# Mixture-of-experts loop: one group of small matmuls per tile, transposes and third weights a tile ahead, routing weights in a row per tile

## The chip, the cores and the metric

One core of a Trainium2 chip. The metric is the device time of one execution in microseconds, median of several runs. The engines that matter are TensorE (PE in the rows, with its weight loads as PEld), VectorE (DVE), ScalarE (ACT) and GpSimd (POOL); SyncE (SP) issues the DMAs. Each engine works through its own list of instructions in order and meets the others at semaphores.

## The reference

Cut to what matters. `x` is 2 x 1024 rows of 256.

```python
x = x + cross_attention(layernorm(x), ctx, ctx, mask)      # 16 heads, 64 keys
# second half, on xf = layernorm(x), 2048 rows:
xa = xf @ P_w.T
C1, C2, C3 = (route(xa, U) for U in (U1, U2, U3))          # per row: softmax of the 3 largest of 12 logits, else 0
mixture = lambda inp, C, W: sum(C[:, e:e+1] * (inp @ W[e].T) for e in range(12))
h = gelu(mixture(xf, C1, W1))
x = x + mixture(h, C2, W2) + C3 @ b2
```

## The kernel before

The 2048 rows are 16 tiles of 128 (T = 16). A first part computes the attention of all tiles and splits the expert weights into a high and a low part of type float32r (`w_h`, `w_l`); a second part, the expert loop, begins some 134 us into the span and is what the change is about. Order and waits are written out by hand, engine by engine; nothing is scheduled by a compiler.

Each product with an expert's weights is made of three matmuls (high x high, low x high, high x low) over two halves of the 256 inputs, six matmuls of 512 columns for two experts at once (a "pair", `expert_pairs`, `split_product`). A layer of a tile has six pairs, so 36 such matmuls; they go to six banks of PSUM in turn. The stationary operand is the tile transposed and split: `xf_h`, `xf_l` for layer 1, `h_h`, `h_l` for layer 2 (the last tile's h goes to `xf_h`, `xf_l`). VectorE multiplies each half bank with its column of routing weights and adds it up (`sum_pair`, L810 and L815: 12 instructions a layer), so a bank is free again once VectorE has read it (semaphore `acc`).

An iteration `experts(t)` on TensorE is: layer 1 of tile t+1, then layer 2 of tile t. Beside the 72 large matmuls it holds small ones in float32, in three places:

- after three pairs of layer 1: two transposes of h(t) (`transpose_h`, L1043) and one of the third routing weights (`transpose_c3`, L1050);
- after six pairs: the bias product with these weights (`expert_bias`, L1055) and two transposes of xf(t+2) (`transpose_xf`, L1025);
- after three pairs of layer 2: the routing logits of tile t+2 (`logits`, L1035: two matmuls, four rows in the trace).

Transposes of h and of xf share one PSUM range, `ps_t`. ScalarE copies the transposes out as high parts (L561, L491, L493), VectorE makes the low parts (`h_low` L751, `xf_low` L746), and TensorE waits for `xf_lo` before layer 1 and for `h_lo` before layer 2.

VectorE, beside the products: `statistics` and `normalise2` of tile t+2 (L595 to L598, L602), `find_top` (L757 to L768: top three and their indices), `combine_weights` (L774 to L793: the dense rows of weights, into `c_new`), `move_weights` (L801: `c_new` to `c_cur`, which layer 2 reads while `c_new` is written anew). GpSimd: `inverse_deviation` (L355, L357: the 1/deviation that `normalise2` waits for), `exponentials` (L406), `split_c3` (L417, L422).

The loop runs over t = 1 to 13 as a hardware loop; t = 0 and t = 14 and the last layer are written out. Inside it, semaphore values and tile offsets are computed in registers by the engine's sequencer (REGISTER_ALU and ISA rows in the order, ALU_OP and FUSED_REGOPS in the trace).

Every on-chip tensor starts at a multiple of 32 bytes, in the order of the declarations. Within 64 bytes `w_h`, `w_l`, `xf_h` and `xf_l` start at 32, `h_h` and `h_l` at 0.

Of the kernel before, what the change touches and what calls it, by code (L numbers as in the profile page):

```python
# [5 lines left out]
ALU = mybir.AluOpType  # L6
# [8 lines left out]
P = 128  # L15
# [6 lines left out]
def xattn_ffn_kernel(nc: bass.Bass, x, mask, ctx_t, wq_t, bq, wk_t, bk, wv_t, bv, wo_t, bo,  # L22
# [56 lines left out]
    with ExitStack() as ctx:  # L79
# [30 lines left out]
        waited = sb("waited", [P, 1])  # L110
        euler = sb("euler", [P, 3 * TOP_K])
# [49 lines left out]
        c_new = sb("c_new", [P, 3, EXPERTS])  # L161
        c_cur = sb("c_cur", [P, 3, EXPERTS])
# [22 lines left out]
        ps_t = banks[:, 5, 0:D].rearrange("p (c t) -> p c t", c=C)  # L185
# [32 lines left out]
        def weights2(t):  # L218

            return c_new if is_last(t) else c_cur  # L220

# [42 lines left out]
        c_moved = sem("c_moved")  # L264
# [56 lines left out]
        def _(pool):  # L321
# [87 lines left out]
            def split_c3(t):  # L409

                if is_last(t):
                    pool.wait_ge(route, ROUTE_STEPS * T)
                else:
                    pool.wait_ge(c_moved, t + 1)
                if later(t, 1):
                    pool.wait_ge(c3t_done, t)
                pool.tensor_tensor(c3_hlh[:, 0:3:2, 0:EXPERTS].bitcast(F32R),  # L417
                                   weights2(t)[:, 2:3, :].to_broadcast([P, 2, EXPERTS]),
                                   ones[:, 0:2 * EXPERTS].rearrange("p (k e) -> p k e", k=2),
                                   ALU.mult).then_inc(c3_hi, 1)  # L420
                pool.wait_ge(c3_hi, t + 1)
                pool.tensor_tensor(c3_hlh[:, 1, 0:EXPERTS], weights2(t)[:, 2, :], c3_hlh[:, 0, 0:EXPERTS],  # L422
                                   ALU.subtract).then_inc(c3_lo, 1)

            exponentials(0)
            inverse_deviation(1, stats2_ready, var2_ready, rstd2_ready)
            exponentials(1)
            split_c3(0)
            with pool.Fori(2, T) as t:
                inverse_deviation(t, stats2_ready, var2_ready, rstd2_ready)  # L430
                exponentials(t)
                split_c3(t - 1)
            split_c3(T - 1)


        @block.scalar
        def _(act):
# [47 lines left out]
            def copy_xf(t):  # L485
# [5 lines left out]
                nc.scalar.activation(xf_t[:, :, :], ps_t, ACT.Copy).then_inc(xf_copied, 1)  # L491
                act.wait_ge(xf_copied, t + 1)
                nc.scalar.activation(xf_h[:, :, :], xf_t[:, :, :], ACT.Copy).then_inc(xf_hi, 1)  # L493
# [55 lines left out]
            copy_xf(0)  # L549
            copy_pt(T - 2)  # L550
# [5 lines left out]
            copy_xf(1)  # L556


            def h_high(t):
                act.wait_ge(ht_done, t + 1)  # L560
                nc.scalar.activation(h_buffers(t)[0][:, :, :], ps_t, ACT.Copy).then_inc(h_hi, 1)  # L561

            def copy_c3t(t):
                act.wait_ge(c3t_done, t + 1)
                nc.scalar.activation(c3_t[:, :], ps_c3, ACT.Copy).then_inc(c3t_copied, 1)
# [7 lines left out]
            gelu(0, SUMS)  # L573

            def experts(t):
# [5 lines left out]
            experts(0)  # L581
            with act.Fori(1, T - 2) as t:
                experts(t)
            h_high(T - 2)
            copy_c3t(T - 2)
            gelu(T - 1, SUMS * 2 * (T - 1))
            h_high(T - 1)
            copy_c3t(T - 1)
# [3 lines left out]
        def _(dve):  # L592
# [155 lines left out]
            def h_low(t):  # L748
                dve.wait_ge(h_hi, t + 1)
                high, low = h_buffers(t)  # L750
                dve.tensor_tensor(low[:, :, :], ps_t, high[:, :, :].bitcast(F32), ALU.subtract).then_inc(h_lo, 1)  # L751

            def find_top(t):

                n = ROUTE_STEPS * t
                dve.wait_ge(z_done, t + 1)
                dve.tensor_copy(z_sb[:, :, :].rearrange("p r e -> p (r e)"), ps_z).then_inc(route, 1)  # L757
# [12 lines left out]
            def combine_weights(t):  # L770
# [20 lines left out]
                if later(t, 1):  # L791
                    dve.wait_ge(c_moved, t)
                dve.tensor_reduce(c_new[:, :, :], w_at_e[:, :, :, :], AX_X, ALU.add).then_inc(route, 1)  # L793

            def move_weights(t):

                dve.wait_ge(route, ROUTE_STEPS * (t + 1))
                if later(t, 1):
                    dve.wait_ge(c3t_done, t)
                    dve.wait_ge(acc, SUMS * (2 * t + 1))  # L800
                dve.tensor_copy(c_cur[:, :, :], c_new[:, :, :]).then_inc(c_moved, 1)  # L801
# [20 lines left out]
            def layer1_pairs(t, pairs, last=True):  # L822
                for pair in pairs:
# [4 lines left out]
                    sum_pair(slot1(t), pair, c_new[:, 0, :], sum1, 0)  # L828
# [3 lines left out]
            def start_layer2(t):  # L832

                dve.wait_ge(y_done, t + 1)
                if is_last(t):
# [3 lines left out]
                if not is_last(t):  # L839
                    dve.wait_ge(c_moved, t + 1)  # L840

            def layer2_pairs(t, pairs):
                for pair in pairs:
                    sum_pair(slot2(t), pair, weights2(t)[:, 1, :], sum2, 1)
# [23 lines left out]
            layer1_pairs(0, range(0, 2))  # L868
            a_low(T - 2)
# [13 lines left out]
            def experts(t, ahead=True):  # L883
                if ahead:
                    statistics(t + 2, x_all, bn2_done, stats2_ready)
# [325 lines left out]
```

## Time and profile before

| | us |
|---|---|
| median of 3 runs | 414.63 (414.23 to 415.75) |
| span of the profiled execution | 412.4 |
| PE busy in it | 392.4 (95%) |
| DVE busy | 342.9 (83%) |
| ACT busy | 115.8 (28%) |
| POOL busy | 110.9 (27%) |

The clock granted to TensorE is full in nearly every slice of the page. Times in the rows are us from the start of the span. A row of the timeline is: start, duration, engine, line, operation, written<-read, count, and in brackets the idle time of the engine before it with what ended it. Instructions overlap on an engine, so the step from one start to the next start is what an instruction takes from the engine's time.

### The profile page before, as it was taken

Reading aid. Unit: us, or ns where it says so; the run is one execution under the profiler, and the core shown is the slowest. Engines: PE = TensorE matmul, PEld = TensorE weight load, DVE = VectorE, ACT = ScalarE, POOL = GpSimd, SP = SyncE. Lnnn points to the kernel's source line nnn. Section 1 sums busy time; section 2 is a strip of 40 time slices with the busy share of each in tenths; the row PEclk is TensorE's granted clock in tenths of the full one; section 3 lists DMA queues with packets and bytes.
Section 4 is the critical chain, followed back from the end, with each engine's and each line's share of the span. In section 5 each row is a group of like instructions: output and inputs, shape, how many; then the busy total and the mean of one; then the engine's idle time right before and its main releaser. Section 6 shows DMA issues by size and latency. Waiting matters only on the chain.

```text
span 412.4 us, 7824 instructions
## 1 busy us (share of the span) xinstructions
PE 392.4 (95%) x2132; PEld 331.0 (80%) x2132; DVE 342.9 (83%) x1036; ACT 115.8 (28%) x263; POOL 110.9 (27%) x165
## 2 busy tenths in 40 slices
PE   4499999999989999999999999999999999999996
PEld 4388988989868888888888888888888888888884
DVE  3998889889885889789897988989789898888875
ACT  3477888888822111010110101011010100101000
POOL 5462755657520220202112020211202112020200
PEclk9999999999989999999999999999999999999999
DMA  7900123131000000000000000000000000000000
GB/s 225 333 2 2 61 92 98 55 102 51 2 0 3 0 2 13 13 0 13 0 13 13 0 13 0 13 0 13 13 0 13 0 13 13 0 13 0 14 0 26
DMA packets 8612, 12.71 MB, mean 31 GB/s; under 512 B 1076, under 2 KB 5016, under 8 KB 8472
## 3 DMA queue, kind: packets, MB, share of 16 engines
q1 hardware_dynamic: 8040, 12.44, 9.1%
q10 hardware_dynamic: 560, 0.13, 0.1%
q8 instruction: 5, 0.08, 0.1%
q14 instruction: 7, 0.06, 0.0%
HBM read 10.47 MB, written 2.10 MB: 30 GB/s over the span
## 4 chain that ended last, share of the span: by engine, by line
PE 89%; DVE 4%; issue 3%; ACT 2%; DMA 1%; POOL 1%; ACTq 0%; DVEq 0%; POOLq 0%
PE banks L920 68%; PE banks L997 5%; PE banks L987 3%; PE banks L962 3%; PE banks L972 2%; PE banks L975 2%; PE banks L977 2%; PE banks L1035 1%; DMA bk_sb<-in_bk_dram 1%; PE banks L1043 1%; DVE q_hl L625 1%; PE banks L1025 1%; PE banks L1008 1%; PE banks L953 1%; DVE s_max L631 1%
## 5 line engine op out<-in xcount | busy, mean ns | idle before, releaser
L815 DVE SCALAR_TENSOR_TENSOR s_d<-banks,c_cur,s_d 128x256 f32<-128x256 f32 x165 | 72.7, 478 | 27.6 <-PE banks L920 23.1
L920 PE MATMUL banks<-w_h,xf_h 128*128 128x512 f32 x204 | 81.8, 401 | 0.0
L920 PE MATMUL banks<-w_l,xf_h 128*128 128x512 f32 x204 | 80.6, 395 | 0.0
L920 PE MATMUL banks<-w_h,xf_l 128*128 128x512 f32 x204 | 80.2, 393 | 0.0
L406 POOL TENSOR_TENSOR top_e<-euler,top_d 128x9 f32<-128x9 f32 x16 | 28.9, 1807 | 185.1 <-DVE top_d L765 185.1
L920 PE MATMUL banks<-w_h,h_h 128*128 128x512 f32 x180 | 73.5, 408 | 0.0
L920 PE MATMUL banks<-w_l,h_h 128*128 128x512 f32 x180 | 71.1, 395 | 0.0
L920 PE MATMUL banks<-w_h,h_l 128*128 128x512 f32 x180 | 71.1, 395 | 0.0
L815 DVE SCALAR_TENSOR_TENSOR sum<-banks,c_new,sum 128x256 f32<-128x256 f32 x160 | 66.6, 476 | 3.2 <-PE banks L920 3.1
L561 ACT ACTIVATE h_h<-banks 128x256 fp32r<-128x256 f32 x15 | 5.8, 385 | 156.5 <-PE banks L1043 156.5
L920 PEld LDWEIGHTS banks<-w_l,xf_h 128*128 128x128 f32 x204 | 38.6, 189 | 8.5
L920 PEld LDWEIGHTS banks<-w_h,xf_l 128*128 128x128 f32 x204 | 38.8, 190 | 7.8
L920 PEld LDWEIGHTS banks<-w_h,xf_h 128*128 128x128 f32 x204 | 38.8, 190 | 7.7
L920 PEld LDWEIGHTS banks<-w_l,h_h 128*128 128x128 f32 x180 | 33.8, 188 | 8.2
L920 PEld LDWEIGHTS banks<-w_h,h_l 128*128 128x128 f32 x180 | 33.9, 188 | 6.9
L920 PEld LDWEIGHTS banks<-w_h,h_h 128*128 128x128 f32 x180 | 33.9, 188 | 6.8
L366 POOL TENSOR_TENSOR w_l<-stage,w_h 128x1024 f32 (+1 forms) x12 | 28.8, 2397 | 32.6 <-ACT w_h L534 32.6
L997 PE MATMUL banks<-v_ext,prob_t 128*128 (+1 forms) x256 | 30.1, 273 | 0.5 <-ACT prob_t L476 0.5
L997 PEld LDWEIGHTS banks<-v_ext,prob_t 128*128 128x128 f32 x256 | 29.9, 192 | 0.7 <-issue 0.7
L571 ACT ACTIVATE xn_t<-xn 128x256 f32<-128x256 f32 x16 | 6.7, 418 | 77.3 <-DVE xn L820 77.3
L631 DVE TENSOR_REDUCE s_max<-banks 128x16 f32<-128x1024 f32 x16 | 19.6, 1223 | 5.6 <-PE banks L977 5.5
L476 ACT ACTIVATE prob_t<-banks 128x512 f32<-128x512 f32 x32 | 17.4, 594 | 17.7 <-PE banks L987 17.6
(126 smaller groups left out, 618.5 us busy)
## 6 DMA issues: line engine op xcount, KB each, us to landing
stage<-in_w_t_dram SPq DMA_DIRECT2D x12, 512.0 KB, 3.7
out_dram<-x_all SPq DMA_DIRECT2D x16, 128.0 KB, 1.9
x_all<-in_x_dram SPq DMA_DIRECT2D x1, 1024.0 KB, 8.0
x_all<-in_x_dram SPq DMA_DIRECT2D x1, 768.0 KB, 7.9
mask_all<-in_mask_dram SPq DMA_DIRECT2D x2, 256.0 KB, 5.1
x_all<-in_x_dram SPq DMA_DIRECT2D x2, 128.0 KB, 3.5
wk_sb<-in_wk_t_dram SPq DMA_DIRECT2D x1, 256.0 KB, 3.7
wq_sb<-in_wq_t_dram SPq DMA_DIRECT2D x1, 256.0 KB, 4.3
```

The costliest lines, as they stand in the source:

```text
L366: pool.tensor_tensor(w_l[:, n, :, :], stage[:, slot, :, :], w_h[:, n, :, :].bitcast(F32), ALU.subtract).then_inc(w_split, 1)
L406: pool.tensor_tensor(top_e[:, :], euler[:, :], top_d[:, :, :].rearrange("p r k -> p (r k)"), ALU.pow).then_inc(e_ready, 1)
L476: nc.scalar.activation(prob_t[:, j:j + HP // 2, :], ps_pt[:, j:j + HP // 2, :], ACT.Copy).then_inc(pt_copied, 1)
L631: dve.tensor_reduce(s_max[:, :], ps_s, AX_X, ALU.max).then_inc(s_maxed, 1)
L815: dve.scalar_tensor_tensor(out=sums[e % 2][:, :], in0=product, scalar=weights[:, e:e + 1], in1=sums[e % 2][:, :], op0=ALU.mult, op1=ALU.ad ...
L920: ins = pe.matmul(dst, a(c), b(c), start=(i == 0), stop=(i == len(terms) - 1))
L962: ins = pe.matmul(ps_q[:, m, :], wq_sb[:, c, m * P:(m + 1) * P], xn_t[:, c, :], start=(c == 0), stop=(c == C - 1))
L972: pe.matmul(banks[:, c, :].rearrange("p (h k) -> p h k", k=KEYS), ident_b[:, :], mask_bias[:, t, :].unsqueeze(1).to_broadcast([P, HPC, KEY ...
L975: pe.matmul(banks[:, c, group * HPG * KEYS:(group + 1) * HPG * KEYS], q_hl[:, c, group, :], kbd_hh[:, b, c, group, :, :].rearrange("p h k ...
L977: ins = pe.matmul(banks[:, c, :], q_h[:, c, :], kbd_l[:, b, c, :, :].rearrange("p h k -> p (h k)"), start=False, stop=True)
L987: ins = pe.transpose(ps_pt[:, j, :], prob[:, 2 * j:2 * j + 2, :].rearrange("p h k -> p (h k)"), ident[:, :])
L997: ins = pe.matmul(ps_v[:, j * 2 * VW:(j + 1) * 2 * VW], prob_t[:, j, :], v_ext[:, b, j, :], start=True, stop=True)
```

## The change

- TensorE: all ten small matmuls of an iteration stand in one place, after three pairs of layer 1: logits of tile t+2, bias product of tile t, transpose of the third weights of tile t+1, transposes of h(t), transposes of xf(t+3). The third weights and xf are thus transposed a tile earlier than before. Layer 2 is no longer interrupted.
- h and xf get halves of a bank of their own (`ps_h`, `ps_xf`).
- `c_new`, `c_cur` and the copy between them go; the routing weights of tile t are written into the row of tile t of `mask_all`, whose masks are no longer needed. The column of weights that `sum_pair` reads is now at an offset that depends on t.
- VectorE: `find_top` moves to behind `h_low`; `statistics` and `normalise2` are of tile t+4 and stand behind `find_top` and behind `combine_weights`; `combine_weights` stands in the middle of layer 2.
- GpSimd: the order is `exponentials(t)`, `split_c3(t)`, `inverse_deviation(t + 2)`. `split_c3` no longer waits for a copy but for the last step of `combine_weights`, and has two small instructions more (`waited_p`) that carry waits.
- ScalarE: `copy_xf` is split in two (`copy_xf`, `xf_high`), and the copy of the third weights is of tile t+1.
- Before the loop stand `transpose_c3(0)` and `transpose_xf(2)` on TensorE and `normalise2(2)`, `statistics(3)`, `normalise2(3)` on VectorE. More iterations are written out at the end.
- The new tensor `waited_p` shifts all that are declared behind it by 32 bytes, and the two that go shift `c3_hlh` and what follows back by 320. Within 64 bytes the weights, `xf_h` and `xf_l` now start at 0, `h_h` and `h_l` at 32.

```diff
@@ gpsimd @@
             def split_c3(t):
-                if is_last(t):
-                    pool.wait_ge(route, ROUTE_STEPS * T)
-                else:
-                    pool.wait_ge(c_moved, t + 1)
+                pool.wait_ge(route, ROUTE_STEPS * (t + 1))
                 if later(t, 1):
                     pool.wait_ge(c3t_done, t)
+                pool.tensor_tensor(waited_p[:, :], ones[:, 0:1], ones[:, 0:1], ALU.mult)
...
-            with pool.Fori(2, T) as t:
-                inverse_deviation(t, stats2_ready, var2_ready, rstd2_ready)
+            with pool.Fori(2, T - 2) as t:
                 exponentials(t)
-                split_c3(t - 1)
-            split_c3(T - 1)
+                split_c3(t)
+                inverse_deviation(t + 2, stats2_ready, var2_ready, rstd2_ready)
@@ scalar @@
+            def experts(t, left):
                 h_high(t)
-                copy_c3t(t)
+                copy_c3t(t + 1)
+                if left > 2:
+                    xf_high(t + 2)
                 gelu(t + 1, SUMS * 2 * (t + 1))
-                copy_xf(t + 2)
+                if left > 3:
+                    copy_xf(t + 3)
@@ vector @@
-                    sum_pair(slot1(t), pair, c_new[:, 0, :], sum1, 0)
+                    sum_pair(slot1(t), pair, combine_row(t, 0), sum1, 0)
...
             layer1_pairs(0, range(0, 2))
+            statistics(2, x_all, bn2_done, stats2_ready)
             a_low(T - 2)
...
             xf_low(1)
             last_sum(0, sum1, h_in[:, :])
+            normalise2(2)
             find_top(1)
-            move_weights(0)
+            statistics(3, x_all, bn2_done, stats2_ready)
             combine_weights(1)
+            normalise2(3)
...
+            def experts(t, left):
                 layer1_pairs(t + 1, range(0, 3))
                 h_low(t)
-                if ahead:
-                    normalise2(t + 2)
+                if left > 2:
+                    find_top(t + 2)
+                if left > 4:
+                    statistics(t + 4, x_all, bn2_done, stats2_ready)
                 layer1_pairs(t + 1, range(3, PAIRS))
                 start_layer2(t)
                 layer2_pairs(t, range(0, 1))
-                if ahead:
+                if left > 2:
                     xf_low(t + 2)
-                layer2_pairs(t, range(1, 4))
-                if ahead:
-                    find_top(t + 2)
+                layer2_pairs(t, range(1, 3))
+                if left > 2:
+                    combine_weights(t + 2)
                 else:
                     h_low(t + 1)
-                layer2_pairs(t, range(4, PAIRS))
-                if ahead:
-                    move_weights(t + 1)
-                    combine_weights(t + 2)
+                if left > 4:
+                    normalise2(t + 4)
+                layer2_pairs(t, range(3, PAIRS))
@@ tensor @@
+            transpose_c3(0)
+            transpose_xf(2)
+            def experts(t, left):
                 pe.wait_ge(xf_lo, t + 2)
                 expert_pairs(slot1(t + 1), range(0, 3), xf_parts, 0)
+                pe.wait_ge(xf_copied, min(t + 3, T) if isinstance(t, int) else t + 3)
+                if left > 2:
+                    logits(t + 2)
+                expert_bias(t)
+                transpose_c3(t + 1)
                 transpose_h(t)
-                transpose_c3(t)
+                if left > 3:
+                    transpose_xf(t + 3)
                 expert_pairs(slot1(t + 1), range(3, PAIRS), xf_parts, 0)
-                expert_bias(t)
                 pe.wait_ge(h_lo, t + 1)
-                if ahead:
-                    transpose_xf(t + 2)
-                expert_pairs(slot2(t), range(0, 3), h_parts, 1)
-                if ahead:
-                    logits(t + 2)
+                if left > 2:
+                    expert_pairs(slot2(t), range(PAIRS), h_parts, 1)
```

TensorE in the loop, around the first place of small matmuls, before:

```order
L920 MATMUL banks<-w_l,xf_h 128x512
L1043 MATMUL banks<-ident,xn_t 128x128 [waits xf_copied,h_ready]
L1043 MATMUL banks<-ident,xn_t 128x128
L1050 MATMUL banks<-ident,c_hlh 96x128 [waits y_added,c3_lo]
L1061 REGISTER_ALU
L920 MATMUL banks<-w_h,xf_h 128x512 [waits acc]
```

and after:

```order
L936 MATMUL banks<-w_l,xf_h 128x512
L1167 REGISTER_ALU
L1053 MATMUL banks<-router_w,xf_t 128x36 [waits y_added,c3t_copied,xf_copied]
L1053 MATMUL banks<-router_w,xf_t 128x36
L1071 MATMUL banks<-b_hhl,c_t 128x256 [waits c3t_copied]
L1066 MATMUL banks<-ident,c_hlh 96x128 [waits c3_lo]
L1061 MATMUL banks<-ident,xn_t 128x128 [waits h_lo,h_ready]
L1061 MATMUL banks<-ident,xn_t 128x128
L1035 REGISTER_ALU
L1041 MATMUL banks<-ident,xf 128x128 [waits xf_copied,xf_ready]
L1041 MATMUL banks<-ident,xf 128x128
L1077 REGISTER_ALU
```

The bias product, the logits and the transposes of xf have moved up here, and the transposes of xf now wait here for `xf_ready`, which VectorE's `normalise2` signals.

GpSimd's loop body before (L355 and L357 are `inverse_deviation`, L417 and L422 `split_c3`):

```order
L355 TENSOR_TENSOR var_eps<-mean_var,eps 128x1 [waits stats2_ready]
L357 TENSOR_TENSOR rstd<-var_eps,minus_half 128x1 [waits var2_ready]
L405 ISA
L406 TENSOR_TENSOR top_e<-euler,top_d 128x9 [waits route]
L416 REGISTER_ALU [waits c_moved]
L417 TENSOR_TENSOR c_hlh<-c_cur,ones 128x2x12 [waits c3t_done]
L422 TENSOR_TENSOR c_hlh<-c_cur,c_hlh 128x12 [waits c3_hi]
```

and after:

```order
L404 TENSOR_TENSOR top_e<-euler,top_d 128x9 [waits route]
L409 ISA
L412 TENSOR_TENSOR waited_p<-ones 128x1 [waits c3t_done,route]
L413 ISA
L413 TENSOR_TENSOR c_hlh<-mask_all,ones 128x2x12
L418 TENSOR_TENSOR waited_p<-ones 128x1 [waits c3_hi]
L419 TENSOR_TENSOR c_hlh<-mask_all,c_hlh 128x12
L352 REGISTER_ALU
L353 TENSOR_TENSOR var_eps<-mean_var,eps 128x1 [waits stats2_ready]
L355 TENSOR_TENSOR rstd<-var_eps,minus_half 128x1 [waits var2_ready]
```

`inverse_deviation` now stands behind `split_c3`, which waits for the end of `combine_weights`.

VectorE in the loop, around `normalise2`, before:

```order
L751 TENSOR_TENSOR h_l<-banks,h_h 128x256 [waits h_hi]
L602 TENSOR_SCALAR xf<-x_all,mean_var,rstd 128x256 [waits rstd2_ready,xft_done]
L806 REGISTER_ALU
L814 REGISTER_ALU [waits pair_done]
L815 SCALAR_TENSOR_TENSOR sum_0<-banks,c_new,sum_0 128x256 [waits acc]
L814 REGISTER_ALU
L815 SCALAR_TENSOR_TENSOR sum_1<-banks,c_new,sum_1 128x256 [waits acc]
```

and after:

```order
L813 ISA [waits route]
L813 TENSOR_REDUCE mask_all<-w_at_e 128x36
L622 TENSOR_SCALAR xf<-x_all,mean_var,rstd 128x256 [waits rstd2_ready,xft_done]
L819 REGISTER_ALU
L827 REGISTER_ALU [waits pair_done]
L828 ISA [waits acc]
L828 SCALAR_TENSOR_TENSOR s_d<-banks,mask_all,s_d 128x256
L827 REGISTER_ALU
L828 ISA [waits acc]
L828 SCALAR_TENSOR_TENSOR s_d<-banks,mask_all,s_d 128x256
```

`normalise2` follows the last step of `combine_weights` at once, and each product has a sequencer instruction more, on which its wait for `acc` now stands.

## Rows read from the trace of the kernel before

**Rows 1.** Waits between 140 and 400 us, all engines: total, times, longest

```profile
DVE s_d L815 <- PE banks L920: 22.6, 32, 1.0
```

**Rows 2.** Chain that ended last, in order of time: start, us, what

```profile
245.41 4.13 PE banks L920 x18
249.87 4.20 PE banks L920 x18
...
263.14 4.12 PE banks L920 x18
...
400.52 8.20 PE banks L920 x36
```

**Rows 3.** Timeline of TensorE, large matmuls around two places of small ones

```profile
262.42 0.39 PE L920 MATMUL banks<-w_l,xf_h 128*128 128x512 f32 x1
...
263.22 0.39 PE L920 MATMUL banks<-w_h,xf_l 128*128 128x512 f32 x1
...
271.42 0.39 PE L920 MATMUL banks<-w_l,h_h 128*128 128x512 f32 x1
...
272.33 0.40 PE L920 MATMUL banks<-w_h,h_l 128*128 128x512 f32 x1
```

**Rows 4.** Timeline of VectorE, one turn of the loop

```profile
260.21 0.18 DVE L801 COPY c_cur<-c_new 128x36 f32<-128x36 f32 x1
260.31 0.27 DVE L774 TENSOR_TENSOR at_e<-top_i,iota_e 128x108 f32<-128x108 uint32 x1
...
261.44 0.27 DVE L793 TENSOR_REDUCE c_new<-w_at_e 128x36 f32<-128x108 f32 x1
261.98 0.43 DVE L595 BATCH_NORM_STATS2 bn<-x_all 128x6 f32 x1 [0.28 <-issue]
...
262.77 0.88 DVE L810 TENSOR_SCALAR sum<-banks,c_new 128x256 f32<-128x256 f32 x2
...
265.13 0.42 DVE L751 TENSOR_TENSOR h_l<-banks,h_h 128x256 fp32r<-128x256 f32 x1
...
265.78 2.49 DVE L815 SCALAR_TENSOR_TENSOR sum<-banks,c_new,sum 128x256 f32<-128x256 f32 x6
268.30 0.42 DVE L820 TENSOR_TENSOR xn<-sum,sum 128x256 f32<-128x256 f32 x1
...
269.22 0.49 DVE L815 SCALAR_TENSOR_TENSOR s_d<-banks,c_cur,s_d 128x256 f32<-128x256 f32 x1 [0.16 <-DVE s_d L837]
...
274.58 0.19 DVE L757 COPY z_sb<-banks 128x36 f32<-128x36 f32 x1
...
275.67 0.86 DVE L815 SCALAR_TENSOR_TENSOR s_d<-banks,c_cur,s_d 128x256 f32<-128x256 f32 x2
```

**Rows 5.** Timeline of GpSimd in the same turn

```profile
260.55 0.23 POOL L417 TENSOR_TENSOR c_hlh<-c_cur,ones 128x24 fp32r<-128x24 f32 x1 [1.09 <-DVE c_cur L801]
260.86 0.21 POOL L422 TENSOR_TENSOR c_hlh<-c_cur,c_hlh 128x12 f32<-128x12 f32 x1
262.71 0.19 POOL L355 TENSOR_TENSOR var_eps<-mean_var,eps 128x1 f32<-128x1 f32 x1 [1.63 <-DVE mean_var L598]
262.98 0.55 POOL L357 TENSOR_TENSOR rstd<-var_eps,minus_half 128x1 f32<-128x1 f32 x1
```

**Rows 6.** Timeline of VectorE before the loop

```profile
112.03 2.00 DVE L746 TENSOR_TENSOR xf_l<-xf_t,xf_h 128x256 fp32r<-128x256 f32 x1
...
133.85 0.42 DVE L820 TENSOR_TENSOR xn<-sum,sum 128x256 f32<-128x256 f32 x1
...
135.60 0.27 DVE L774 TENSOR_TENSOR at_e<-top_i,iota_e 128x108 f32<-128x108 uint32 x1
...
137.98 0.27 DVE L793 TENSOR_REDUCE c_new<-w_at_e 128x36 f32<-128x108 f32 x1
```

**Rows 7.** Timeline of TensorE, first large matmul of tile 1

```profile
134.18 0.48 PE L920 MATMUL banks<-w_h,xf_h 128*128 128x512 f32 x1
```

**Rows 8.** Timeline of GpSimd, exponentials of tile 1

```profile
135.22 1.81 POOL L406 TENSOR_TENSOR top_e<-euler,top_d 128x9 f32<-128x9 f32 x1 [15.07 <-DVE top_d L765]
```

More of the change, by code:

```diff
@@ L110, in xattn_ffn_kernel @@
         waited = sb("waited", [P, 1])
+        waited_p = sb("waited_p", [P, 1])
         euler = sb("euler", [P, 3 * TOP_K])
@@ L426, in _ @@
             inverse_deviation(1, stats2_ready, var2_ready, rstd2_ready)
+            split_c3(0)
+            inverse_deviation(2, stats2_ready, var2_ready, rstd2_ready)
             exponentials(1)
-            split_c3(0)
-            with pool.Fori(2, T) as t:
-                inverse_deviation(t, stats2_ready, var2_ready, rstd2_ready)
+            split_c3(1)
+            inverse_deviation(3, stats2_ready, var2_ready, rstd2_ready)
+            with pool.Fori(2, T - 2) as t:
                 exponentials(t)
-                split_c3(t - 1)
-            split_c3(T - 1)
+                split_c3(t)
+                inverse_deviation(t + 2, stats2_ready, var2_ready, rstd2_ready)
+            for t in range(T - 2, T):
+                exponentials(t)
+                split_c3(t)
         @block.scalar
@@ L490, in copy_xf, with xf_high @@
                     act.wait_ge(xf_lo, t)
-                nc.scalar.activation(xf_t[:, :, :], ps_t, ACT.Copy).then_inc(xf_copied, 1)
+                if later(t, 3):
+                    act.wait_ge(h_lo, t - 2)
+                nc.scalar.activation(xf_t[:, :, :], ps_xf, ACT.Copy).then_inc(xf_copied, 1)
+            def xf_high(t):
                 act.wait_ge(xf_copied, t + 1)
+                if later(t, 1):
+                    act.wait_ge(pair_done, PAIRS * slot1(t - 1) + PAIRS)
                 nc.scalar.activation(xf_h[:, :, :], xf_t[:, :, :], ACT.Copy).then_inc(xf_hi, 1)
@@ L756, in find_top @@
                 dve.wait_ge(z_done, t + 1)
+                if later(t, 1):
+                    dve.wait_ge(c3t_done, t)
                 dve.tensor_copy(z_sb[:, :, :].rearrange("p r e -> p (r e)"), ps_z).then_inc(route, 1)
@@ L790, in combine_weights @@
                 dve.wait_ge(route, n + 5)
[L791 to L801, printed above, removed]
+                dve.tensor_reduce(mask_all[:, t, 0:ROUTES].bitcast(F32).rearrange("p (r e) -> p r e", r=3),
+                                  w_at_e[:, :, :, :], AX_X, ALU.add).then_inc(route, 1)
             def sum_pair(slot, pair, weights, sums, added):
@@ L834, in start_layer2 @@
                 dve.wait_ge(y_done, t + 1)
+                dve.wait_ge(c3t_copied, t + 1 if is_last(t) else t + 2)
                 if is_last(t):
@@ L1019, in transpose_xf @@
                 pe.wait_ge(xf_ready, t + 1)
-                if later(t, 2):
-                    pe.wait_ge(h_lo, t - 1)
+                if later(t, 1):
+                    pe.wait_ge(xf_copied, t)
                 else:
-                    pe.wait_ge(xf_copied if t else xt_copied, 1 if t else T)
+                    pe.wait_ge(xt_copied, T)
                 for c in range(C):
-                    ins = pe.transpose(ps_t[:, c, :], xf[:, c * P:(c + 1) * P], ident[:, :])
+                    ins = pe.transpose(ps_xf[:, c, :], xf[:, c * P:(c + 1) * P], ident[:, :])
                 ins.then_inc(xft_done, 1)
@@ L1039, in transpose_h @@
                 pe.wait_ge(h_ready, t + 1)
-                n = min(t + 2, T) if isinstance(t, int) else t + 2
-                pe.wait_ge(xf_copied, n)
+                if later(t, 1):
+                    pe.wait_ge(h_lo, t)
                 for c in range(C):
-                    ins = pe.transpose(ps_t[:, c, :], h[:, c * P:(c + 1) * P], ident[:, :])
+                    ins = pe.transpose(ps_h[:, c, :], h[:, c * P:(c + 1) * P], ident[:, :])
                 ins.then_inc(ht_done, 1)
```

84 lines of the change are left out of this document (44 added, 40 removed).

## The prediction

> **What bounds the kernel now.** I read the page first, then the waits of the expert part, then the chain that ended last, then each engine's timeline over one turn of the loop. The page shows TensorE busy nearly throughout; the list of waits between 140 and 400 us settles what that means, since TensorE is not in it at all. Its longest entry on VectorE is VectorE waiting for TensorE, 22.6 us in 32 pieces [rows 1]. So in the loop TensorE is the bound, and no wait that is removed on another engine can gain anything. A turn of the loop takes 17.73 us (263.14 less 245.41) [rows 2]. It holds 72 large matmuls, 18 of them in 4.13 or 4.20 us, and ten small ones. A gain must therefore make TensorE's own list shorter or faster; a loss comes when another engine takes longer than 17.73 us a turn, or when TensorE must stop.
>
> **The small matmuls in one place.** The change neither removes nor adds a matmul; the question is whether a place of small ones costs something beyond its members. From the large matmul before a place to the second one behind it, 0.80 us pass where three small ones stand and 0.91 us where four stand [rows 3]. Two steps of 0.23 us (4.13 us over 18) [rows 2] belong to the large ones, which leaves 0.34 and 0.45 us: 0.11 us for each small one both times, and nothing fixed. Ten in one place then cost the same 1.1 us a turn as in three places. I take 0 for this term; the bound on the gain is what rounding hides, 0.02 us for each of two places in 14 turns, 0.6 us, and I see no reason for a loss.
>
> **Waits on TensorE in the loop.** The third weights, xf(t+3) and the logits' input are made a whole turn earlier, so their transposes find them ready if the other engines keep up; h(t) is transposed where it was. Cost 0 in the loop.
>
> **Before the loop TensorE has to stop twice.** This is the term I can size. First, `transpose_xf(2)` now stands ahead of layer 1 of tile 1 and needs `normalise2(2)`, which VectorE does one step behind the last sum of tile 0: that sum starts at 133.85 [rows 6], the next instruction some 0.34 us later at 134.19 (two of this size take 0.65 in the loop [rows 4]), and it takes 0.41, so xf is there at about 134.65. TensorE would be there at 134.18 [rows 7] plus 0.11 for the third weights, 134.29: a stop of 0.4 us. Second, in `experts(0)` it needs `normalise2(3)`. The last step of `combine_weights(1)` ends at 138.25 [rows 6], now somewhat later for the inserted `normalise2(2)`, between 0 and its 0.33; 0.13 taken, since VectorE idled before `find_top`: 138.38. Then GpSimd does `split_c3(1)` and only then `inverse_deviation(3)`: 0.16 us from VectorE's result to GpSimd's start (260.39 to 260.55) [rows 4, 5], 0.31 and 0.21 for the two splits, 0.19 for each of two `waited_p` (the row of an instruction on one column), 0.27 and 0.55 for the deviation [rows 5], in all 1.88 us. With 0.41 for the normalising, xf(3) is there at 140.7. TensorE starts tile 1 at 134.9 (134.29, the stop, two transposes), needs 4.2 us for 18 large matmuls [rows 2] and 0.85 us for the eight small rows ahead: 139.95. A stop of 0.75 us. Together 1.15 us; if the two `waited_p` are free it is 0.8, if they take 0.3 each 1.4. `statistics(2)`, put ahead of `a_low(T - 2)`, falls into idle time of VectorE and costs nothing.
>
> **What VectorE has to do in a turn.** Its list gets a wait inside: `normalise2(t+4)` stands directly behind `combine_weights(t+2)`, and its deviation comes from GpSimd behind `split_c3(t+2)`, which waits for that same `combine_weights`. Queued behind the wait are the products of the last three pairs; waiting for these, in the end, is TensorE, at `h_lo` of the next turn. The sum, as steps from start to start [rows 4]: three pairs of layer 1, 262.77 to 265.13, 2.36; `h_low` and `normalise2`, 0.65; the other three pairs, 2.52; to the first product of layer 2, 0.92; `find_top`, 274.58 to 275.67, 1.09; `statistics` between its 0.43 and the 0.79 up to the next row, 0.6 taken; `combine_weights`, 260.31 to 261.44 and 0.27 more, 1.40; twelve products of layer 2 at 0.39, 4.72; `xf_low` like half of the 0.65, 0.33; last sum and the loop's branch, 0.42 and 0.28. That is 15.3 us. The wait adds the 1.88 of above: 17.2 us. Then the offsets in registers. Each product has a sequencer instruction more, and its wait for `acc` stands on that. From a result to the start of a product behind such an instruction the row at 269.22 shows 0.16 us. Two products back is 0.78 us of start, 0.48 of duration, so 0.30 us are left for 0.16: between products it is hidden, by 0.14 us. It is not hidden where the list resumes: at the loop's start (three such instructions), at the start of layer 2 and at the last step of `combine_weights`. Bounds are 0 and five times 0.16, 0.8 us; I take 0.5. VectorE then needs 17.7 us, within 17.2 to 18.0, against TensorE's 17.73. The 1.6 us a turn in which VectorE waited (22.6 over 14 turns [rows 1]) are used up, but just not exceeded. Where VectorE falls short by little, the banks give room: `h_low` may be some 2 us late before TensorE stops, beside the delay of the first turn. So 13 turns that are too long by x cost 13x less 2 us, and nothing up to 0.15 us.
>
> **The sum.** 1.15 us on the profiled 412.4 gives 413.55; the median of the runs lies 2.2 us above the profiled span, so 415.8 us, 0.3% slower. What this kernel's measurement can tell from no change is about 0.5%, 2.1 us. The forecast's own range is 414.8 to 416.7.
>
> **Rival: VectorE becomes the bound.** This is the one that ends slower. It decides from x = 0.24 us a turn (13 times 0.24 less 2 is 1.1, with the stops 2.2 us). My sum has 17.7 with 0.3 of doubt on either side, and the costs that I could not see in the rows, sequencer instructions, lie all on this side. With x = 0.4, the time is 415.8 + 3.2 = 419.0; with 0.6, 421.6. For it speaks how near the two sums are; against it that the idle time found [rows 1] understates the room, since two instructions in a row overlap (0.48 us long, 0.39 apart) and a wait between them hides that.
>
> **Rival: the port between VectorE and GpSimd.** VectorE's `xf_low` took 2.00 us at 112.03, beside GpSimd's subtraction on the weights, where such an instruction else takes 0.4 [rows 4, 6]. `exponentials`, 1.81 us, now falls beside `statistics`. If GpSimd held VectorE up there, `statistics` would wait some 1.5 us, and 13 turns of 1.5 less 2 make 17.5 us: 433 us. But the comparison at 135.60 ran wholly beside `exponentials` of tile 1 and took 0.27, as without it at 260.31 [rows 4, 6, 8]. The Trainium skill (SBUF — State Buffer, Terms) says that the two engines share a port pair, held for the full instruction, and the loser blocks; by that the first row is explained and this rival would come true, and the second row speaks against it for this instruction.
>
> **Rival: the large matmuls change their pace.** In layer 2 the loop's matmuls go at 4.20 us for 18, 0.2333 each; in the last layer 2 of all, which uses `xf_h` and `xf_l` as stationary operand, 36 take 8.20, 0.2278 each [rows 2]. Work and banks are the same, the buffer is not: it starts at 32 bytes within 64 like the weights, `h_h` at 0. The change makes it weights and xf at 0, h at 32. If pace goes with the pair's difference, nothing changes, which I take. If it goes with the absolute place of the stationary operand, h gets faster and xf slower, and the sum is near 0. If all reach 0.2278, 15 layers of 36 gain 5.5 ns each, 3.0 us: 412.8, and even this only if VectorE's turn is shorter than I think. If all go at 0.2333, 16 layers of 36 lose up to 5.5 ns, 3 us: 418.8.
>
> **Rival: the stops are covered.** If TensorE comes to them later than I think, the time is 414.6.
>
> **How the numbers follow.** Forecast 0.48; VectorE the bound, enough to be seen, 0.32; pace slower 0.06; port 0.03; stops covered 0.04; pace faster 0.07. Slower by over 0.5% hold the second to fourth, 0.41; faster, beyond 412.6, is at most the last, mostly short of it: 0.05; the rest, 0.54, is within. The range goes from 412.5 to 421.5 us: it takes in the paces, the stops and an x up to 0.6, and leaves out the port and the worst of x, some 0.15.
>
> **What would show it.** Right: TensorE absent from the waits of the loop, two stops of 0.4 and 0.75 us before 141 us at the transposes of xf, and on VectorE a wait of about 1.9 us a turn for `rstd`. VectorE the bound: a wait of TensorE for `h_l` in every turn from some turn on, and a turn over 17.75. Pace: the 36 matmuls of layer 2 in other than 8.4 us. Wrong altogether would be a turn shorter than 17.6 us with the pace unchanged: then a place of small matmuls does have a cost of its own, which two rows here deny.

## The result, and the profile after

| | before | after |
|---|---|---|
| median of the runs of this comparison, us | 414.24 (16 runs, 413.94 to 415.76) | 415.45 (16 runs, 414.99 to 416.98) |
| profiled span, us | 412.4 | 413.7 |
| a turn of the loop, us | 17.75 | 17.75 |
| from the logits of tile 1 to the last pair of sums, us | 275.01 | 276.17 |

The ratio is 1.0025, with an interval of 1.0014 to 1.0037: 0.25% slower, where 0.3% was forecast. The median of 415.45 us lies 0.35 us under the forecast of 415.8, because 16 runs put the kernel before at 414.24 us where the forecast had started from 414.63. The last line of the table is a stretch that I use throughout. It begins with TensorE's logits of tile 1, the last work ahead of everything that the change moves, and ends where VectorE starts the last two products of all. The time ahead of it differs by up to 1.7 us between executions, whatever the kernel (133.74 to 135.39 us in the profiles below), so tenths of a microsecond are read from the stretch and not from the medians. Here are its two ends, from the timeline and the chain of before, and then the same two of after (start us, us, what):

```profile
133.74 0.61 PE L1035 MATMUL banks<-router_w,xf_t 128*128 128x36 f32 x4 [0.61 <-DVE x_all L662]
408.75 0.89 DVE s_d L815 x2
```

```profile
133.86 0.60 PE L1053 MATMUL banks<-router_w,xf_t 128*128 128x36 f32 x4 [0.61 <-DVE x_all L682]
410.03 0.89 DVE s_d L828 x2
```

The page of after shows the same number of matmuls (2132) and TensorE as busy as before:

```profile
span 413.7 us, 8095 instructions
PE 394.1 (95%) x2132; PEld 332.9 (80%) x2132; DVE 337.1 (81%) x1021; ACT 118.9 (29%) x263; POOL 114.8 (28%) x197
```

The waits of after between 140 and 400 us (total, times, longest), without ScalarE's. They answer to [rows 1]:

```profile
POOL waited_p L412 <- DVE mask_all L813: 98.6, 14, 7.2
POOL top_e L404 <- DVE top_d L787: 98.3, 14, 7.7
...
DVE xf L622 <- POOL rstd L355: 23.2, 13, 1.8
...
DVE sum L828 <- PE banks L936: 4.2, 9, 0.6
DVE sum L823 <- issue: 4.2, 10, 0.4
DVE s_d L828 <- PE banks L936: 3.3, 7, 0.5
...
PEld banks L1041 <- DVE xf L622: 0.8, 1, 0.8
PE banks L1041 <- DVE xf L622: 0.6, 1, 0.6
```

TensorE waits once, at 140.8 us, for `xf`, and never in the loop. VectorE waited 22.6 us for TensorE before; now it waits 23.2 us for GpSimd's `rstd`, 1.8 us in each of 13 turns. One wait took the place of the other.

The chain of after, in order of time. It answers to [rows 2]:

```profile
157.91 0.37 PE banks L1053 x4
159.02 16.63 PE banks L936 x72
175.65 0.37 PE banks L1053 x4
...
370.92 0.37 PE banks L1053 x4
...
388.91 8.33 PE banks L936 x36
397.58 12.42 PE banks L936 x54
```

From 157.91 to 370.92 there are 12 turns: 17.75 us each, as before. The 1.16 us that the stretch gained must lie outside the loop. The timeline of TensorE ahead of the loop shows them (start, us, in brackets the idle time ahead of the instruction and who ended it):

```profile
134.30 0.29 PE L1066 MATMUL banks<-ident,c_hlh 128*96 128x128 f32 x1
134.77 0.44 PE L1041 MATMUL banks<-ident,xf 128*128 128x128 f32 x2 [0.17 <-DVE xf L622]
...
139.52 0.37 PE L1071 MATMUL banks<-b_hhl,c_t 96*128 96x256 f32 x1
139.73 0.28 PE L1066 MATMUL banks<-ident,c_hlh 128*96 128x128 f32 x1
139.84 0.38 PE L1061 MATMUL banks<-ident,xn_t 128*128 128x128 f32 x2
140.81 0.44 PE L1041 MATMUL banks<-ident,xf 128*128 128x128 f32 x2 [0.59 <-DVE xf L622]
```

From start to start 0.47 us pass at the first place, where one small matmul takes 0.11: a stop of 0.36 us. At the second 0.97 us pass, where the two transposes of `h` take 0.22: a stop of 0.75. Together 1.11 us, of the 1.16 that are to be explained.

### The profile page after: what moved, and what is told of

It reads as the page before. It is cut to its first block, busy times and chain, and to the rows that moved or that the text cites. A ratio compares the mean times of both kernels' runs of the same rounds, so it can differ in the third digit from the quotient of the medians.

```text
span 413.7 us, 8095 instructions
## 1 busy us (share of the span) xinstructions
PE 394.1 (95%) x2132; PEld 332.9 (80%) x2132; DVE 337.1 (81%) x1021; ACT 118.9 (29%) x263; POOL 114.8 (28%) x197
## 4 chain that ended last, share of the span: by engine, by line
PE 87%; issue 5%; DVE 4%; ACT 1%; DMA 1%; POOL 1%; ACTq 0%; DVEq 0%; POOLq 0%
PE banks L936 65%; PE banks L1013 5%; PE banks L978 3%; PE banks L1003 3%; PE banks L988 2%; PE banks L991 2%; PE banks L993 2%; PE banks L1053 1%; DMA bk_sb<-in_bk_dram 1%; PE banks L1061 1%; PE banks L1041 1%; PE banks L969 1%; PE banks L1024 1%; PE banks L1071 1%; DVE q_hl L645 1%
## 5 line engine op out<-in xcount | busy, mean ns | idle before, releaser
L828 DVE SCALAR_TENSOR_TENSOR s_d<-banks,mask_all,s_d 128x256 f32<-128x256 f32 x176 | 75.2, 478 | 9.9 <-PE banks L936 6.3
L828 DVE SCALAR_TENSOR_TENSOR sum<-banks,mask_all,sum 128x256 f32<-128x256 f32 x160 | 66.5, 477 | 7.3 <-PE banks L936 5.9
L936 PE MATMUL banks<-w_h,h_h 128*128 128x512 f32 x180 | 71.5, 397 | 0.0
L412 POOL TENSOR_TENSOR waited_p<-ones 128x1 f32<-128x1 f32 x16 | 3.2, 200 | 100.4 <-DVE mask_all L813 100.4
L622 DVE TENSOR_SCALAR xf<-x_all,mean_var,rstd 128x256 f32 (+1 forms) x16 | 6.6, 413 | 24.0 <-POOL rstd L355 24.0
```

The source lines that it names most:

```text
L622: dve.tensor_scalar(dst[:, :], src[:, t, :], mean_var[:, 0:1], rstd[:, 0:1], ALU.subtract, ALU.mult).then_inc(ready, 1)
L828: dve.scalar_tensor_tensor(out=sums[e % 2][:, :], in0=product, scalar=weights[:, e:e + 1], in1=sums[e % 2][:, :], op0=ALU.mult, op1=ALU.ad ...
L936: ins = pe.matmul(dst, a(c), b(c), start=(i == 0), stop=(i == len(terms) - 1))
```

## Experiments on the two stops and on VectorE's room

**The stops taken away (head).** The transposes of xf(2) go behind the first pair of layer 1, and GpSimd makes the deviation of tile 3 before it splits tile 1's third weights.

```
             exponentials(1)
-            split_c3(1)
             inverse_deviation(3, stats2_ready, var2_ready, rstd2_ready)
+            split_c3(1)
...
-            transpose_xf(2)
...
-                expert_pairs(slot1(t + 1), range(0, 3), xf_parts, 0)
+                expert_pairs(slot1(t + 1), range(0, 1), xf_parts, 0)
+                if isinstance(t, int) and t == 0:
+                    transpose_xf(2)
+                expert_pairs(slot1(t + 1), range(1, 3), xf_parts, 0)
```

> The changed kernel with its two stops of TensorE before the loop taken away: the transposes of xf(2) stand behind the first pair of layer 1 of tile 1 instead of ahead of it, and GpSimd makes the deviation of tile 3 before it splits the third weights of tile 1. The loop is untouched. My theory (the 1.2 us of the change are these stops, and nothing in the loop costs or gains): 0.8 to 1.2 us less than the changed kernel, 414.4 us, and no wait of TensorE before 141 us. Rival (the loss lies in the loop or at its end, and the stops are absorbed by later slack): no change, 415.4 us.

Measured: 414.81 us, ratio to before 1.0011 (0.9995 to 1.0027), where the changed kernel has 1.0025. All ratios are to runs of the kernel before on the same chip at the same time, whose medians were 414.24, 414.14 and 414.27 us for the three groups of runs. The stretch fell from 276.17 to 275.27 us, that is by 0.90, and the turn stayed at 17.75 us. It still is 0.26 us above before, and one stop of TensorE before 141 us is left, which the expectation had denied. The timeline shows it:

```profile
139.50 0.36 PE L1071 MATMUL banks<-b_hhl,c_t 96*128 96x256 f32 x1
139.94 0.31 PE L1066 MATMUL banks<-ident,c_hlh 128*96 128x128 f32 x1
```

0.44 us lie between these two, against 0.20 in a turn of the loop (264.62 and 264.82 in the changed kernel). The third weights of tile 1 are now split last and come 0.24 us too late. One stop of 0.75 us was exchanged for one of 0.24. So the loss of the change lies in stops ahead of the loop: 0.90 us went with them, and this one accounts for nearly all of the rest. The two edits were not run apart.

**GpSimd's order changed in the loop too (order).** In addition to the edit above:

```
                 exponentials(t)
-                split_c3(t)
                 inverse_deviation(t + 2, stats2_ready, var2_ready, rstd2_ready)
+                split_c3(t)
```

> As the run before, and in the loop too GpSimd makes the deviation of tile t+2 before it splits the third weights of tile t, so that VectorE's wait of 1.8 us a turn inside its list goes. My theory (TensorE bounds the loop at 17.75 us a turn, VectorE only just keeps up): no further gain, 414.4 us, a turn of 17.75 us, and VectorE's 1.8 us a turn come back as waits for TensorE's banks. Rival (VectorE bounds the turn, and its equality with TensorE's list is no accident): a turn shorter by some tenths, 13 times 0.1 to 0.3 us, 411 to 413 us.

Measured: 414.52 us, ratio 1.0005 (0.9987 to 1.0022), stretch 275.27 us, exactly as with the stops alone, turn 17.75 us. VectorE's wait for `rstd` is gone, and its waits for others grew:

```profile
DVE sum L828 <- PE banks L936: 10.8, 23, 0.6
DVE s_d L828 <- PE banks L936: 7.0, 20, 0.5
DVE h_l L771 <- ACT h_h L574: 6.1, 13, 0.7
```

The turn did not get shorter without this wait, so VectorE was not the bound. But how near was it? The waits don't tell: 23.2 us went and only about 16 came back here. The next four runs measure the room.

**Work added to VectorE (after_load1, after_load3, before_load3, order_load3).** One or three additions of 256 columns a turn, into buffers that nobody reads any more, ahead of `start_layer2(t)`:

```
+                for n in range(1):
+                    dve.tensor_tensor((a_n[:, :], ...)[n], bo_sb[:, :], bv_sb[:, :], ALU.add)
                 start_layer2(t)
```

> The changed kernel with one more instruction on VectorE in each of 15 turns, an addition of 256 columns whose result nobody reads, ahead of the start of layer 2: about 0.35 us a turn. My theory (VectorE needs 17.7 of TensorE's 17.75 us): x is 0.3 us, 13 times 0.3 less 2 is 1.9 us, 417.4 us, with waits of TensorE for h_l late in the loop. Rival (VectorE has more room than its short waits tell): 415.4 us, and TensorE stays out of the waits.

> As the run before with three such instructions, about 1.05 us a turn. My theory: x is 1.0 us, 13 times 1.0 less 2 is 11 us, 426 us, a turn of 18.7 us from the second or third on. Rival with 0.5 us of room: x is 0.5, 4.5 us, 420 us. No change at all would mean that VectorE has over 1 us of room a turn and that my sum of its list was 1 us too long.

Measured: with one, 416.05 us, ratio 1.0044 (1.0028 to 1.0061), but a stretch of 276.18 us, the same as without it. With three, 423.10 us, ratio 1.0209 (1.0192 to 1.0227), stretch 283.91 us, 7.7 more. Both expectations of my theory missed: 417.4 us with waits of TensorE for one, where the rival (no wait, no loss) came true, and 426 us for three, which was 3 us too high. The timelines show what goes on in both. First the kernel with one addition: when `h_l` is made, and when TensorE starts layer 2 with it, nine turns apart:

```profile
179.54 0.41 DVE L771 TENSOR_TENSOR h_l<-banks,h_h 128x256 fp32r<-128x256 f32 x1
...
182.14 0.39 PE L938 MATMUL banks<-w_h,h_h 128*128 128x512 f32 x1
...
341.28 0.41 DVE L771 TENSOR_TENSOR h_l<-banks,h_h 128x256 fp32r<-128x256 f32 x1
...
341.90 0.44 PE L938 MATMUL banks<-w_h,h_h 128*128 128x512 f32 x1
```

VectorE's turn is (341.28 - 179.54) / 9 = 17.97 us, TensorE's 17.75. `h_l` is ready 2.19 us ahead of TensorE at first and 0.21 us at the end: the room that the banks give is used up and the loop ends just before anything stops. Then with three additions, a late turn:

```profile
199.41 0.41 DVE L771 TENSOR_TENSOR h_l<-banks,h_h 128x256 fp32r<-128x256 f32 x1
...
348.48 0.41 DVE L771 TENSOR_TENSOR h_l<-banks,h_h 128x256 fp32r<-128x256 f32 x1
...
349.04 0.49 PE L938 MATMUL banks<-w_h,h_h 128*128 128x512 f32 x1 [0.65 <-DVE h_l L771]
```

VectorE's turn is (348.48 - 199.41) / 8 = 18.63 us, and TensorE waits for `h_l` in each. Two more additions cost 0.66 us, one 0.33. So without any, VectorE needs 17.97 - 0.33 = 17.64 us. It has 0.11 us of room a turn, and my sum of its list had said 17.7.

> The kernel before with the three added VectorE instructions a turn, at the same place. Each was worth 0.335 us in the changed kernel (turns of 17.97 with one and 18.64 us with three), so 1.0 us a turn. My theory: the kernel before has some 1.6 us a turn in which VectorE waits for TensorE, so nothing changes: 414.2 us, a turn of 17.75 us. Rival (the kernel before had no more room than the changed one, and the order of VectorE's list did not matter): 8 us more, as in the changed kernel, 422 us.

> The changed kernel with the stops removed and GpSimd's deviation ahead of its split in the loop, and the three added instructions a turn. VectorE's list would be 17.63 less the wait of 1.8 plus 1.0, 16.8 us. My theory: the room that the change took lies wholly in that wait, so 414.5 us and a turn of 17.75 us, no change. Rival (the wait only moved into the list of VectorE elsewhere, and the room is still 0.1 us): a turn of 18.6 us, 422 us.

Measured: before with three additions 414.36 us, ratio 0.9997 (0.9979 to 1.0015), stretch 274.99 us (275.01 without). VectorE's wait for TensorE there fell from 22.6 us to 11.6:

```profile
DVE s_d L815 <- PE banks L922: 11.6, 15, 0.9
```

The kernel order with three: 414.71 us, ratio 1.0006 (0.999 to 1.0022), stretch 275.28 us (275.27 without). Both have at least the 1.0 us of room a turn that was added. The changed kernel has 0.11, and in the loop the order of three GpSimd steps is all that the kernel order has different from it.

## Experiments on the pace of the large matmuls

A large matmul has a stationary operand (`xf_h`, `xf_l`, `h_h` or `h_l`) and a moving one (`w_h` or `w_l`). The runs shift the first against the second by a few unused bytes, with no instruction changed:

```
+        pad_h_h = sb("pad_h_h", [P, 8])
         h_h = sb("h_h", [P, C, P], F32R)
```

with 8, 24, 40 or 56 elements of 4 bytes, and for the run with xf the same line ahead of `xf_h`.

> The kernel before with 32 unused bytes a partition ahead of h_h and h_l, so that they start at the same place modulo 64 bytes as the weights they are multiplied with; no instruction is changed. Theory A (the pace of a large matmul goes with the difference of the two operands' places): layer 2 goes at the pace of layer 1, some 0.228 instead of 0.2333 us each, 15 times 36 times 5.5 ns is 3.0 us less, 411.3 us. Theory B (the pace goes with the layer, by the weights or the banks that it uses): no change, 414.3 us.

> The changed kernel with the same 32 bytes ahead of h_h and h_l, so that weights, xf and h all start at 0 modulo 64. Theory A (pace by the difference): TensorE's turn falls to 17.55 us; VectorE, which needs about 17.7, then falls behind by up to 0.2 us a turn, which the banks cover for most of the 13 turns, so 412.5 to 413.5 us. Theory B (no effect of the place): 415.4 us. If instead it is the absolute place of the left operand, h at 0 stays slow and nothing changes here while the same bytes help the kernel before.

> The kernel before with 96 unused bytes ahead of h_h and h_l instead of 32: the distance from the weights to h_h is then a multiple of 256 bytes, as it is for xf_h. With 32 bytes (distance a multiple of 64, not of 256) the turn fell from 17.75 to 17.61 us and layer 2 from 0.2333 to about 0.2294 us a large matmul; layer 1, with xf_h, goes at 0.2279. Theory A2 (the distance counts modulo 256): layer 2 at 0.2279 too, a turn of 17.55 us, 411.0 us. Theory A (modulo 64 alone): as with 32 bytes, 17.61 us and 411.9 us.

> The kernel before with 32 unused bytes ahead of xf_h: xf_h and xf_l now stand 32 bytes off the weights modulo 64, and h_h and h_l, which lie behind them, come to the same place as in the run with 32 bytes ahead of h_h. If pace goes with the distance of the buffer from the weights, the two layers change places: layer 1 at 0.233 to 0.234 us, layer 2 at 0.2294, a turn of 17.82 us, 415 us. If pace goes with the layer or with where h stands alone, layer 1 stays at 0.228 and the time is 411.9 us.

> The kernel before with 224 unused bytes ahead of h_h: the distance from the weights is then 128 more than a multiple of 256, as in the changed kernel with 32 bytes, where layer 2 went at 0.2324 us. If the distance modulo 256 decides, layer 2 at about 0.232 and a turn of 17.7 us, 413.5 us. If it is the distance modulo 64 and the changed kernel differs for another reason, layer 2 at 0.229 and 411.7 us.

> The kernel of the run named order with 160 unused bytes ahead of h_h, so that its distance from the weights is a multiple of 256 bytes. By the distance modulo 256 TensorE's turn is 17.56 us as in the kernel before with 96 bytes, and with both stops gone the time 411.6 us: equal to that one, and grouping is worth nothing. If grouping gained what rounding hides, up to 0.6 us, 411.0. If VectorE had been the bound at 17.63, the turn would stay there and the time be 412.5.

Distances are those from `w_h` to the buffer, modulo 256 bytes, in the layout of the program. The column of layer 2 is read between starts in the timeline at about 270 us: of the 18 behind the logits for the kernels built on before (its first step is some 0.09 us longer, behind small matmuls), of all 36 for the others.

| run | h_h from w_h | xf_h from w_h | layer 2, us | turn, us | stretch, us | median, us | ratio to before |
|---|---|---|---|---|---|---|---|
| before | 160 | 0 | 4.29 | 17.75 | 275.01 | 414.24 | |
| before_pad | 192 | 0 | 4.22 | 17.61 | 272.85 | 411.88 | 0.9933 (0.9908 to 0.9957) |
| before_pad96 | 0 | 0 | 4.21 | 17.56 | 272.12 | 411.54 | 0.9945 (0.9932 to 0.9959) |
| before_pad224 | 128 | 0 | 4.27 | 17.71 | 274.34 | 413.78 | 0.9986 (0.9970 to 1.0001) |
| before_xf_off | 192 | 32 | 4.21 | 17.79 | 275.73 | 415.04 | 1.0030 (1.0013 to 1.0047) |
| after | 96 | 0 | 8.43 | 17.75 | 276.17 | 415.45 | 1.0025 (1.0014 to 1.0037) |
| after_pad | 128 | 0 | 8.37 | 17.67 | 274.98 | 414.26 | 1.0003 (0.9987 to 1.0019) |
| order | 96 | 0 | 8.43 | 17.75 | 275.27 | 414.52 | 1.0005 (0.9987 to 1.0022) |
| order_pad160 | 0 | 0 | 8.16 | 17.46 | 270.93 | 410.26 | 0.9901 (0.9875 to 0.9926) |

Thirty-two bytes of nothing make the kernel before 0.7% faster. Theory B, that pace goes with the layer, has fallen. In before_xf_off layer 1 is the slow one: its 18 from 276.71 to 280.92 us take 4.21 us, against 4.13 in before (276.30 to 280.43). Absolute place has fallen too: `xf_h` is fast at 32 within 64 (before) and at 0 (after). What all nine agree with is the distance between the two operands. It isn't the clock: between 150 and 370 us the granted clock is 1.00 in before, before_pad96, after and order_pad160 alike. A distance of 0 modulo 256 is the fastest, 192 is near it, and 128, 160, 96 and 32 are slow. Modulo 64, which I had assumed, isn't enough: 128 bytes off is 0 modulo 64 and yet slow, in two kernels. Why the distance matters the runs don't tell, and nothing between these six distances was tried. The changed kernel with 32 bytes missed its expectation of 412.5 to 413.5 us for this reason, since 128 was taken to be as good as 0; VectorE did not hold it back.

**The fastest kernel, order_pad160, also gives a figure for grouping.** It and before_pad96 have both distances at 0 and differ by 0.10 us a turn, 1.2 us in the stretch; the expectation had been equality. Every sixth large matmul behind the logits in before_pad96, from the timeline of TensorE (the fourth is the first of layer 1):

```profile
270.96 0.48 PE L921 MATMUL banks<-w_h,h_h 128*128 128x512 f32 x1
...
272.43 0.40 PE L921 MATMUL banks<-w_h,h_h 128*128 128x512 f32 x1
...
273.81 0.39 PE L921 MATMUL banks<-w_h,h_h 128*128 128x512 f32 x1
...
275.17 0.39 PE L921 MATMUL banks<-w_h,xf_h 128*128 128x512 f32 x1
```

The same in order_pad160, first from the place of ten on and then in layer 2:

```profile
262.43 0.48 PE L937 MATMUL banks<-w_h,xf_h 128*128 128x512 f32 x1
...
263.89 0.39 PE L937 MATMUL banks<-w_h,xf_h 128*128 128x512 f32 x1
...
265.25 0.39 PE L937 MATMUL banks<-w_h,xf_h 128*128 128x512 f32 x1
...
266.61 0.39 PE L937 MATMUL banks<-w_h,h_h 128*128 128x512 f32 x1
...
267.97 0.39 PE L937 MATMUL banks<-w_h,h_h 128*128 128x512 f32 x1
```

Six settled ones take 1.36 us, 0.2267 each. Behind the place of the logits above, the first six take 1.47 and the second six 1.38; behind the other two places of before_pad96 the same timeline gives 1.48 and 1.36, and 1.46 and 1.37. Of each first six 0.09 us is the longer step of the very first one, which the 0.11 us for each small matmul already hold. Over 1.36 and that, the three places have 0.09 us too much together, and the one place of order_pad160 (1.46, then 1.36) has 0.01. That is 0.08 of the 0.10 us a turn (0.07 in the mean of 12 turns). So a place does have a small price, paid by the large matmuls behind it. In the changed kernel two things hide it. Its layer 2 never gets to 1.36, with or without a place:

```profile
269.46 0.39 PE L936 MATMUL banks<-w_h,h_h 128*128 128x512 f32 x1
...
270.86 0.40 PE L936 MATMUL banks<-w_h,h_h 128*128 128x512 f32 x1
...
272.27 0.40 PE L936 MATMUL banks<-w_h,h_h 128*128 128x512 f32 x1
```

Six take 1.40 and 1.41 there, with no small matmul near. And its distance of 96 is a little slower than the 160 of before: in the mean of the turns, from start to start, the large matmuls of layer 2 take 0.05 us a turn more in after than in before, and everything else in the turn 0.05 us less. order_pad160 is 1.0% faster than before. By the stretches 2.9 us of its 4.1 are those that 96 bytes gave the kernel before, and 1.2 came with the grouped order, in spite of a stop of about 0.26 us that is left in it. These two also differ in VectorE's and GpSimd's order and in where all the buffers lie; but TensorE waits for neither engine in the loop of either kernel, and the settled pace of six is 1.36 us in both. No run groups the small matmuls and changes nothing else, so the part of the 1.2 us that the rows behind the places don't account for is put down to grouping without a test.

## Why the prediction was right, point by point

**The bound.** TensorE is absent from the waits of the loop, as said, and stayed so with one addition on VectorE.

**Small matmuls in one place, 0.** The turn stayed at 17.75 us, but partly by luck: layer 2 lost 0.05 us a turn by its new distance, and the rest of the turn gained as much. As a rule it is wrong. From the large matmul ahead of the place of ten, at 264.03, to the second behind it, at 265.60, 1.57 us pass; less 0.46 this is 0.11 for each of the ten, the figure that came out of [rows 3]:

```profile
264.03 0.39 PE L936 MATMUL banks<-w_l,xf_h 128*128 128x512 f32 x1
264.25 0.53 PE L1053 MATMUL banks<-router_w,xf_t 128*128 128x36 f32 x4
...
265.28 0.48 PE L936 MATMUL banks<-w_h,xf_h 128*128 128x512 f32 x1
265.60 0.40 PE L936 MATMUL banks<-w_h,xf_l 128*128 128x512 f32 x1
```

The step of the prediction that failed is "and nothing fixed", with its bound of 0.6 us. I looked at the two large matmuls beside a place and not at the ten behind it. Where the buffers let the pace settle, the gain that came with grouping is 1.2 us, twice the bound.

**Two stops, 0.4 and 0.75 us.** Measured 0.36 and 0.75, and the stretch grew by 1.16 us against a forecast of 1.15. The first was worked out carelessly: 134.19 and 0.41 make 134.60, not 134.65, and so a stop of 0.31 us where the prediction has 0.4. The sum does not suffer from it, since the second stop ends when xf(3) is there and grows by what the first one lacks. In the second one small errors cancelled: `combine_weights(1)` ended at 138.57 and not at 138.38, GpSimd's chain took less than 1.88 us, and TensorE came 0.1 us later than I had it. VectorE's rows show 1.77 us from 138.57 to the start of the normalising:

```profile
138.30 0.27 DVE L813 TENSOR_REDUCE mask_all<-w_at_e 128x36 f32<-128x108 f32 x1
...
140.34 0.41 DVE L622 TENSOR_SCALAR xf<-x_all,mean_var,rstd 128x256 f32<-128x256 f32 x1 [1.78 <-POOL rstd L355]
```

**VectorE's list, 17.7 us within 17.2 to 18.0.** Measured 17.64, by the added work. (Twelve products at 0.39 are 4.68 and not 4.72, which changes nothing here.) The 2 us of delay that the whole loop may gather before TensorE stops were somewhat low: in after `h_l` is ready about 2.7 us ahead of TensorE's start, turn for turn, and in after_load3, where TensorE waits for it, 0.15 us ahead, so there are 2.5. In after_load1 the margin fell by 2.0 us and nothing stopped. The rule made of it, 13x less 2, was too high. For x = 0.22 it gives 0.9 us, and 0.0 was measured; for x = 0.88 (18.63 less 17.75) it gives 9.4, and 7.7 was measured. It took 13 turns to be too long. In after_load3 the steps of VectorE from one `h_l` to the next show ten of 18.63 to 18.66 us, then one of 18.13 and one of 14.90, so the last turns, which hold fewer of VectorE's steps, don't count. TensorE's turns there are one of 17.99, eight of 18.60 to 18.66 and one of 18.15, which over 17.75 makes the 7.7.

**The rival of VectorE as the bound** (0.32) didn't come true. It was the right one to fear: the distance was 0.11 us a turn, and the trace of after alone doesn't show on which side it lies.

**The port.** It didn't come true either. GpSimd's exponentials and VectorE's `statistics` of the same turn, from their timelines:

```profile
267.54 1.81 POOL L404 TENSOR_TENSOR top_e<-euler,top_d 128x9 f32<-128x9 f32 x1 [7.28 <-DVE top_d L787]
```

```profile
267.81 0.41 DVE L615 BATCH_NORM_STATS2 bn<-x_all 128x6 f32 x1
```

The second ran wholly beside the first and took 0.41 us, against 0.43 with GpSimd idle in [rows 4, 5]. So the lock on which this rival was built, one for any two instructions of these engines, did not hold these two up.

**Pace.** That it goes with the difference of the pair, the case that I took, is what the runs show. That the change leaves the difference alone is not: it does so modulo 64 only, and modulo 256 the difference went from 160 bytes to 96. Both happen to be slow, which was luck: layer 2's 36 take 8.43 us where 8.4 were named. What I mis-sized is the prize: 3.0 us from equal buffers became 2.9 in the kernel before and 4.3 with the grouped order.

## What to carry over

When the busiest engine is full and another needs nearly as long, add a known dose of work to the second one. A wait list shows how long an engine waited, not how much it could have taken: 23.2 us of waiting hid a room of 0.11 us a turn. Before instructions are moved in a stream of matmuls, compare the steps of six in a row of each kind. Where the same shape has two paces, shift one buffer first; here that was worth 2.9 us in the kernel before, against the 1.2 that came with the reordering, and the slow distance hid the latter.

## What the runs showed of the hardware

- The pace of a stream of 128x512 matmuls on fp32r, with a new stationary operand for each, depends on the distance between the two operands' buffers: 0.2267 us each at 0 modulo 256 bytes, 0.2325 at 128, 0.2342 at 96, at a granted clock of 1.00. The table above has the other three distances, and why the distance matters is not known. The Trainium skill (TensorE: Matmul & The Clock Gate, Step-by-step: what each phase is for) says that TensorE has two independent read ports and that loading the next weights doesn't steal bandwidth from the running matmul. Nothing in that would make the distance matter; the measurement decides, and here it does matter.
- Where both operands' distance is 0, the pace settles only some six to twelve large matmuls after small ones: 1.46, then 1.36 us for six, or 1.47, 1.38 and 1.36, of which 0.09 us is the longer first step.
- An addition of 256 columns on VectorE with all operands in SBUF costs 0.33 us of its time in a row of others, though it is shown as 0.41 or 0.42 us long.
